# Attention stage: shorter rsqrt chains, one masking of the keys' sums, and the first choices' gating on ScalarE

## The reference, cut to what matters

```python
x = x + 0.5 * ffn(layernorm(x))     # 8 experts, top 2 of a softmax, capacity 1024 rows each
x = x + attention(layernorm(x))     # linear attention, 16 heads of 8
x = x + 0.5 * ffn(layernorm(x))
# attention:
q = elu(x @ Wq.T + bq) + 1; k = elu(x @ Wk.T + bk) + 1; v = x @ Wv.T + bv
kv = einsum('bthd,bthe->bhde', k, v)
denom = einsum('bthd,bhd->bth', q, k.sum(axis=1))
num = einsum('bthd,bhde->bthe', q, kv)
out = (num / clip(denom, 1e-6)) @ Wo.T + bo
# end of ffn: each token takes back the rows of its two experts, each by its gate
out = sum(gate[..., None] * y[topi, pos_c], axis=1)
```

## Time and profile before

| what | us |
|---|---|
| median of the three runs shown | 529.95 (525.56 to 532.13) |
| profiled execution, its own time | 536.02 |
| its span, from first to last instruction | 534.2 |
| VectorE busy | 351.1 (66%) |
| TensorE matmuls busy | 350.5 (66%) |
| ScalarE busy | 236.3 (44%) |
| GpSimd busy | 270.0 (51%) |
| mean granted clock of TensorE | 0.827 of full |

### The profile page before, as it was taken

How to read it: one execution, slowest core, us unless ns; L and a number is a source line. 1 busy time by engine, 2 the same in 40 slices (tenths; PEclk the granted TensorE clock), 3 DMA queues, 4 the chain that set the end, 5 groups by cost and what they waited for, 6 DMA issues and landing times. The chain is left out here.

```text
span 534.2 us, 6016 instructions
## 1 busy us (share of the span) xinstructions
PE 350.5 (66%) x1705; PEld 285.3 (53%) x1705; DVE 351.1 (66%) x1110; ACT 236.3 (44%) x431; POOL 270.0 (51%) x302
## 2 busy tenths in 40 slices
PE   7815568999999144887772466500088999999700
PEld 7803357888887023666651355400086888888500
DVE  6797448988887264678771585720016899999674
ACT  3685326677765022543550272310015666667400
POOL 8001765665531574554567114557720676766740
PEclk9999997999999655976785598555578999999955
DMA  8911113666652411111111001111140222321299
GB/s 244 360 48 39 51 50 121 209 224 214 222 203 88 123 51 34 39 42 34 39 48 60 17 6 41 39 41 58 58 159 1 80 83 90 88 82 44 64 341 299
DMA packets 44688, 55.22 MB, mean 103 GB/s; under 512 B 6678, under 2 KB 28208, under 8 KB 44656
## 3 DMA queue, kind: packets, MB, share of 16 engines
q1 hardware_dynamic: 31776, 35.14, 19.7%
q0 software_dynamic: 8512, 17.60, 11.4%
q10 hardware_dynamic: 4368, 2.10, 1.3%
HBM read 25.98 MB, written 28.84 MB: 103 GB/s over the span
## 5 line engine op out<-in xcount | busy, mean ns | idle before, releaser
L1060 ACT ACTIVATE hf<-psum,bcol 128x512 f32<-128x512 f32 x128 | 88.5, 692 | 74.0 <-PE psum L997 50.4
L966 POOL DMA_INDIRECT xg<-xn_dram,gidx x64 | 64.6, 1010 | 75.9 <-POOLq L1634 39.5
L956 POOL DMA_INDIRECT yt_dram<-y_sb,target x64 | 71.3, 1114 | 51.4 <-DVE y_sb L1113 30.3
L1097 DVE TENSOR_TENSOR hl<-hf,hh 128x512 fp32r<-128x512 f32 x128 | 87.7, 697 | 7.9 <-ACT hh L1062 4.7
L1202 POOL DMA_INDIRECT yg<-y_dram,slot x64 | 60.9, 951 | 62.8 <-DVE x_sb L1436 22.9
L801 POOL DMA_INDIRECT xs_dram<-xns,place x64 | 62.0, 969 | 53.2 <-DVE xns L788 34.6
L1086 DVE TENSOR_TENSOR xl<-psum,xh 128x512 fp32r<-128x512 f32 x32 | 21.9, 685 | 55.8 <-ACT xh L1045 55.8
L993 PE MATMUL psum<-xh,wres 128*128 128x512 f32 x128 | 54.3, 424 | 4.0 <-ACT xh L1045 2.7
L1008 PE MATMUL psum<-hh,wres 128*128 128x512 f32 x128 | 53.3, 416 | 0.0
L997 PE MATMUL psum<-xl,wres 128*128 128x512 f32 x128 | 51.9, 405 | 0.8 <-DVE xl L1086 0.7
L1090 DVE CAST hh<-hf 128x512 fp32r<-128x512 f32 x96 | 43.7, 455 | 11.8 <-issue 5.8
(11 more groups left out here) (232 smaller groups left out, 740.4 us busy)
## 6 DMA issues: line engine op xcount, KB each, us to landing
yt_dram<-zeros SPq DMA_DIRECT2D x24, 256.0 KB
ring<-yt_dram SPq DMA_DIRECT2D x24, 256.0 KB
xs_dram<-zeros SPq DMA_DIRECT2D x16, 288.0 KB
xg<-xs_dram SPq DMA_DIRECT2D x16, 288.0 KB
wexp_raw<-in_L_ffn_w SPq DMA_DIRECT2D x16, 256.0 KB, 6.3
y_dram<-y_sb SPq DMA_DIRECT2D x16, 256.0 KB
x_sb<-in_L_attn_x SPq DMA_DIRECT2D x8, 256.0 KB, 4.0
xn_dram<-xns SPq DMA_DIRECT2D x8, 256.0 KB, 6.1
```

The costliest lines, as they stand in the source:

```text
L956: gp.indirect_dma_start(out=yt_dram, out_offset=bass.IndirectOffsetOnAxis(ap=target[:, j:j + 1], axis=0), in_=self.y_sb[:, s % YG, t], in_ ...
L966: gp.indirect_dma_start(out=self.xg[:, s % 4, t], out_offset=None, in_=xn_dram, in_offset=bass.IndirectOffsetOnAxis(ap=gidx[:, j:j + 1], a ...
L1060: one = nc.scalar.activation(self.hf[:, c], bank[1 + c][:], ACT.Relu, bias=bcol[:, at:at + 1])
L1097: dve.tensor_tensor(self.hl[:, s % 2, c], self.hf[:, c], self.hh[:, s % 2, c].bitcast(F32), ALU.subtract).then_inc(hl_ready[c], 1)
```

## The change

Four edits, all of them around the attention stage:

1. Both rsqrt chains make one Newton turn (three instructions) and one third-order turn (four) in place of three Newton turns (nine). In the scale's chain the constants differ, as it holds minus an eighth of the root's inverse.
2. The tile of values `vv` gets 16 columns of ones in place of one, the matmul of the keys' sums has 144 columns in place of 129, `block_mask` holds the mask of the heads beside the mask of the blocks, and one instruction of 144 columns masks both. `query` waits for one signal of it, not for two.
3. ScalarE multiplies the first choices' rows of groups 1 to 7 by their gates, in place (`gated_firsts(s + 1)`, right behind `anT_out(s)`; it waits for the rows' arrival). VectorE then adds a whole group in one instruction of 512 columns, and waits for ScalarE's signal `yg_gated`. The signal that frees the rows' buffer (`yg_used[0]`) still comes from the addition. Group 0 stays as it was.
4. In VectorE's list `add_rows(s + 1, 0)` moves behind `residual(s - 2)` and `statistics(s - 2)`.

```diff
-            for turn in range(3):
-                ch.add(dve.tensor_tensor(a, y, y, ALU.mult))
+            for turn in range(2):
+                if turn == 0:
+                    ch.add(dve.tensor_tensor(a, y, y, ALU.mult))
+                else:
+                    ch.add(dve.scalar_tensor_tensor(a, y, LAST_SQUARE, y, ALU.mult, ALU.mult))
...
+                if turn == 1:
+                    ch.add(dve.scalar_tensor_tensor(a, a, LAST_SHIFT, a, ALU.add, ALU.mult))
...
-                ch.add(dve.scalar_tensor_tensor(rstd[:, ts] if turn == 2 else y, a, 1.5, y, ALU.add, ALU.mult))
+                ch.add(dve.scalar_tensor_tensor(rstd[:, ts] if turn == 1 else y, a, 1.875 if turn == 1 else 1.5, y, ALU.add, ALU.mult))
...
-                    pe.wait_ge(kv_masked, 2 * n + 2)
+                    pe.wait_ge(kv_masked, n + 1)
...
+                def gated_firsts(n):
+
+                    act.wait_ge(yg_in[0][n % YB], 64 * (n // YB + 1))
+                    for t in range(GT):
+                        at = GT * n + t
+                        y = self.yg[:, n % YB, 0, t]
+                        last = nc.scalar.activation(y, y, ACT.Identity, scale=gate[:, 0, at:at + 1])
+                    last.then_inc(yg_gated, 1)
...
                     if s < NG:
                         anT_out(s)
+                    if s + 1 < NG:
+                        gated_firsts(s + 1)
...
+                    if k == 0 and n > 0:
+                        xb = x_sb[:, GT * n:GT * n + GT]
+                        dve.wait_ge(yg_gated, n)
+                        dve.tensor_tensor(xb, self.yg[:, n % YB, k], xb, ALU.add).then_inc(yg_used[k], 1)
+                        return
...
-                    for square in (64.0, 16.0, 4.0):
+                    for square in (64.0, KEY_SQUARE):
...
-                    dve.tensor_tensor(self.kv[:, u, 0:C], bank[4][:, 0:C], block_mask[:], ALU.mult).then_inc(kv_masked, 1)
-                    dve.tensor_tensor(self.kv[:, u, C:C + HEADS], head_mask[:], bank[4][:, C:C + 1].to_broadcast([P, HEADS]), ALU.mult).then_inc(kv_masked, 1)
+                    dve.tensor_tensor(self.kv[:, u], bank[4][:, 0:C + HEADS], block_mask[:], ALU.mult).then_inc(kv_masked, 1)
...
-                    if s + 1 < NG:
-                        add_rows(s + 1, 0)
                     if s >= 2:
                         residual(s - 2)
                         statistics(s - 2)
+                    if s + 1 < NG:
+                        add_rows(s + 1, 0)
```

More of the change, by code:

```diff
@@ L58 @@
 RSQRT_SEED = 1597463007.0
+LAST_SQUARE, LAST_SHIFT = 1.2247449159622192, 2.041241407394409
+KEY_SQUARE, KEY_SHIFT = 19.595918655395508, -4.082482814788818
 NEG_EIGHTH_SEED = RSQRT_SEED - 3 * 2.0 ** 23 - 2.0 ** 31
@@ L138, in macaron @@
         head_mask = sb("head_mask", [P, HEADS])
-        block_mask = sb("block_mask", [P, P])
+        block_mask = sb("block_mask", [P, C + HEADS])
         zeros = sb("zeros", [P, GT, XW])
@@ L239, in macaron @@
         yg_used = sems("yg_used", 2)
+        yg_gated = sem("yg_gated")
         xs_cleared = sem("xs_cleared")
@@ L295, in row_scalar_steps @@
                 ch.wait(done)
-                ch.add(dve.scalar_tensor_tensor(rstd[:, ts] if turn == 2 else y, a, 1.5, y, ALU.add, ALU.mult))
+                if turn == 1:
+                    ch.add(dve.scalar_tensor_tensor(a, a, LAST_SHIFT, a, ALU.add, ALU.mult))
+                    done = ch.n
+                    yield
+                    ch.wait(done)
+                ch.add(dve.scalar_tensor_tensor(rstd[:, ts] if turn == 1 else y, a, 1.875 if turn == 1 else 1.5, y, ALU.add, ALU.mult))
                 done = ch.n
@@ L1231, in __init__ @@
                 self.kk = new("kk", [P, 2, GT, C])
-                self.vv = new("vv", [P, 2, GT, C + 1])
+                self.vv = new("vv", [P, 2, GT, C + HEADS])
                 self.kv = new("kv", [P, 2, C + HEADS])
@@ L1277, in keysum @@
                     for t in range(GT):
-                        last = nc.tensor.matmul(bank[4][:, 0:C + 1], self.kk[:, n % 2, t], self.vv[:, n % 2, t], start=(t == 0), stop=(t == GT - 1))
+                        last = nc.tensor.matmul(bank[4][:, 0:C + HEADS], self.kk[:, n % 2, t], self.vv[:, n % 2, t], start=(t == 0), stop=(t == GT - 1))
                     last.then_inc(keysum_ready, 1)
                 def query(n):
-                    pe.wait_ge(kv_masked, 2 * n + 2)
+                    pe.wait_ge(kv_masked, n + 1)
                     pe.wait_ge(qT_ready, n + 1)
@@ L1474, in scale_steps @@
                         ch.wait(done)
-                        to = self.rsa[:, u, 0] if square == 4.0 else y
-                        ch.add(dve.scalar_tensor_tensor(to, a, -3.0, y, ALU.add, ALU.mult))
+                        if square == KEY_SQUARE:
+                            ch.add(dve.scalar_tensor_tensor(a, a, KEY_SHIFT, a, ALU.add, ALU.mult))
+                            done = ch.n
+                            yield
+                            ch.wait(done)
+                            ch.add(dve.scalar_tensor_tensor(self.rsa[:, u, 0], a, 7.5, y, ALU.add, ALU.mult))
+                        else:
+                            ch.add(dve.scalar_tensor_tensor(y, a, -3.0, y, ALU.add, ALU.mult))
                         done = ch.n
@@ L1670, in _ @@
                 ch.then(nc.gpsimd.affine_select(out=head_mask[:], in_=head_mask[:], compare_op=ALU.is_ge, fill=0.0, base=HD - 1, pattern=[[HD, HEADS]], channel_multiplier=-1))
[L1671 removed]
+                ch.add(nc.gpsimd.tensor_copy(block_mask[:, C:C + HEADS], head_mask[:]))
+                ch.add(nc.gpsimd.tensor_copy(block_mask[:, 0:C].rearrange("p (h d) -> p h d", d=HD), head_mask[:].unsqueeze(2).to_broadcast([P, HEADS, HD])))
                 ch.add(nc.gpsimd.iota(iota_lo[:], pattern=[[1, P]], base=0, channel_multiplier=0, **fl))
@@ L1770, in _ @@
             def _(gp):
-                nc.gpsimd.memset(attention.vv[:, :, :, C:C + 1], 1.0).then_inc(ones_col, 1)
+                nc.gpsimd.memset(attention.vv[:, :, :, C:C + HEADS], 1.0).then_inc(ones_col, 1)
                 route1.last_column(gp)
```

## The result

The changed kernel takes 538.62 us (median of 4 runs, 537.80 to 540.53) against 531.04 us for the kernel before (4 runs, 525.56 to 538.14): ratio 1.0165, 95% interval 1.0122 to 1.0208. Without it the median before is 529.95 us, and the change costs 8.7 us. It is slower; whether by more or less than 2% the interval leaves open. The profiled execution took 539.17 us, its span is 537.4 us at a granted clock of 0.825; before it was 536.02 and 534.2. So the two traces differ by 3.2 us where the times differ by 8.7: the profiled execution of before is slower than those three runs. What a faster execution of it looks like on that chip stands in no trace.

The account below looks back on a forecast made before the run. It took attention-stage turns to be bound by a ring of GpSimd gathers and late TensorE signals. 4.8 + 2.0 - 2.0 + 1.4 - 1.0 = +5.2 us, factor 1.0097, on the median 529.95 is 535.1 us; range 522 to 543.

Parts of the forecast that it names:

- the case that I called likeliest: Whole kernel: the forecast's own case, 532 to 538 us, likeliest 535, chance 0.42.
- A sign of being wrong: Attention stage: the prediction is wrong if TensorE's keys' sums are seen at once while GpSimd gathers.
- the ring: Attention stage: addition, eight gathers and late TensorE signal close a loop, 13.15 us a turn becoming 14.35, +4.8 in all.
- The first turn: Addition for group 2: now waits for ScalarE's copy and multiplications; +2.0 us taken, bounds 0 and 4.6.
- The dispatch: First dispatch: GpSimd's wait of 1.99 us before the last four gathers goes, -2.0 us.
- Behind the stall: After the first dispatch's wait: group 7's addition and the second choices come 3.3 us later, 1.9 taken back, +1.4 us.
- Rsqrt: Shorter chains outside the ring: 0.3 us in the first routing, 0.7 in the second routing's last parts, -1.0.
- the other one of the prediction: Attention stage: the addition must follow ScalarE's copy 0.60, multiplications 1.27 and hand-over 0.05 us.
- VectorE's length as the pace: Attention stage: turns as long as VectorE's list, saving 7.8 us, 522; halfway or nothing seen, 524 to 532, chance 0.28.
- The stall at the dispatch: First dispatch: a wait costing up to 13 us goes, giving 517 to 522 us; chance 0.12.
- The stronger ring: Attention stage: the ring plus 3 us from second-routing logits held by bursts, +10.8 or +12.3, 541 to 542; chance 0.18.

Follow-up runs that it names:

- the fast chip: Either of the two chips used for the first eight follow-up runs; the kernel before takes 497 us there.
- the two small parts: Shorter rsqrt chains and the single masking only, against the kernel before: 494.21 us, ratio 0.9932.
- the slow chip: The chip used for the last four follow-up runs; the kernel before takes 536.02 us there.
- the shorter addition: Shorter rsqrt chains, single masking, one-instruction addition in old place, no gate multiplication for first choices of groups 1 to 7, against the kernel before: 535.58 us, ratio 1.0021.
- the long burst: Shorter rsqrt chains, single masking, GpSimd's gathers waiting only for the buffer they write, against the kernel before: 542.06 us, ratio 1.0143.
- the move alone: Only the first choices' addition moved behind the residual and the statistics, against the kernel before: 501.38 us, ratio 1.0077.
- the gating alone: Only ScalarE multiplying the first choices' rows and VectorE's one-instruction addition, in its old place, against the kernel before: 517.06 us, ratio 1.0399.

## Why the forecast came out as it did

I forecast 535.0 us and 1.0097 times the kernel before; it is 538.62 us and 1.0165. The time is in the range, but 0.6 us above the 532 to 538 of the case that I called likeliest, in which the forecast lay. The change costs 8.7 us where I forecast 5.2, and the cause is only half of the story.

*A sign of being wrong that came.* I had written that the prediction is wrong if the keys' sums are seen at once while GpSimd gathers. They are: they end at 230.34 and the masking starts at 230.38, while the gathers run from 223.40 to 233.15, and in the turn before at 216.06 and 216.31. What the trace bears out is narrower than that test: signals given 6.8 and 6.9 us into these bursts pass, and those given 8.3 to 9.7 us into them are seen only behind the end. So the ring closes through the projection and the transposition, and not through the masking. Nor was VectorE idle 1 to 4 us for ScalarE in these turns: it was 0.25, since the residual's own late signal came first.

*The ring.* Forecast 14.35 us a turn, measured 14.12 in the turns for groups 3 and 4. The parts: addition 0.69, hand-over 0.27, gathers 9.75, until the signal 1.62, copy 0.50 (the multiplications start 0.50 behind its start, I had counted its whole 0.60), multiplications 1.26, hand-over 0.03. So +0.97 a turn; then +1.18 for group 5 and +0.40 for group 6, in which I had counted the full 1.20 although the bound of 0 for the last two was written beside it. Measured over four turns +3.5, forecast +4.8.

*The first turn.* I took +2.0; the addition for group 2 starts at 208.32, before at 208.35: 0. I had left out that group 1's addition also waits for ScalarE, 4.68 us, and starts at 195.23 in place of 191.19; the gathers start later, `anT_out(1)` comes at 206.53, earlier than the 211.00 of the earlier trace rows, and the two cancel.

*The dispatch.* -2.0 forecast; the scatters start 1.38 us later than before, which is +3.5 less 2.1. Right. With the two errors above, 278.19 in place of my 281.6.

*Behind the stall.* +1.4 forecast; from 1.38 us later at the first dispatch to 3.75 at the second part's first scatter it is +2.4. The residual and `anT_out(6)` go on together at 302.04 and 302.09, 3.7 us behind the last scatter's end at 298.31 (before 1.1 for the residual and 3.3 for the copy), and the addition and the second choices behind them, as I had it, only later.

*Rsqrt.* -1.0 forecast; from the second part's scatters to the fourth's (354.16, before 351.32) the difference falls from 3.75 to 2.84, -0.9. Some 0.4 comes back behind them. On the fast chip, where no late signal covers the chains, the two small parts are worth 3.3 us. That is more than the 1.0 of the sum, and less than the 4.7 that it would be with 0.4 and 0.06 more in each of 8 groups.

*The sum.* +5.2 forecast, the traces give 537.44 - 534.18 = +3.3. The times give +8.7, and the interval's lower end, 1.0122, lies above my 1.0097. That 538.62 is near 535 is thus partly luck: the sum of the terms, made against one execution of a kernel whose runs spread over 12.6 us, is too small. Of the 8.7 us the traces account for 3.3; for the rest there is no trace, and which term it belongs to stays open.

*The cause.* "The ring of gathers and late signals" describes the slow chip: the turn of before, 12.71 with the shorter addition, the 12.7 us of the long burst, and the two turns of 14.12 at granted clocks of 0.96 and 0.76 fit it. As the reason for the change's price it isn't needed: on the fast chip, without one late signal, the change costs 1.82%, and with half of the gathers gone 1.28%, against 1.65% in the result. In both places the turn can come to nearly the same length, 14.12 and 14.20 us, and up to the keys' sums it is the same (they start 228.95 - 222.44 = 6.51 us behind the addition in one, 217.12 - 210.61 = 6.51 in the other). What fills it up differs: on the fast chip it is TensorE's slow matmuls, without which the turn is 11.52; on the slow one it is late signals, with 2.6 us of it beyond TensorE's own end at a clock of 0.96, and with 0.85 us where its matmuls are slow as well. That the two lengths agree is chance. The step common to both is the other one of the prediction: the addition can't start before `anT_out`, the multiplications and the hand-over. Moving the multiplications ahead of the copy took back 6.4 of 9.2 us on the fast chip. What is left there, 1.0065 against the 0.9932 of the two small parts alone, isn't taken apart; the move alone had cost 0.8%. The term that I had in no list at all is TensorE's clock, 0.76 where the turn takes 14.2 us there and 0.96 where it takes 11.5.

*The rivals.* VectorE's length as the pace was to make it faster when signals aren't late; on the fast chip they weren't, and it was slower, since the idle time before the addition isn't VectorE's length. I had weighed the wait for ScalarE against it as a matter of chance, where it decides. The stall at the dispatch stayed. The stronger ring, at 541 to 542, did not come. ScalarE, busy less than half of the span, gave 1.26 us a turn and cost VectorE up to 5.0 in the run with the gating alone. The Trainium skill (ScalarE: Activation LUTs, Rules for kernel authors) gives multiplications and additions to VectorE; by the time, the runs agree with it (1.0399 for the gating alone), though for the place of the work more than for its price, 1.26 us on ScalarE against 0.44 saved.

## What to carry to other kernels

Before work is moved to an idle engine, look at what stands ahead of it in that engine's list and what that waits for: 1.26 us of work placed behind a copy that depends on the same turn's matmuls made a loop through three engines out of an addition that had waited for neither of the other two. Then try the place before the amount: the same instructions two positions earlier in the list were 1.3% faster. And a wait for a remote signal, read from one trace, may not be the kernel's: price the change without it as well, before a forecast rests on it. Last, when two orders are compared by one turn, look at its neighbours and at the granted clock in each: here the same kernel's turn was 11.52 and then 14.20 us.

## What was unexpected of the hardware

The same kernel took 531 us beside the result, 497 us beside the first eight runs and 536 us beside the last four. Nearly the whole difference lies ahead of the last scatter: from there to the end it is 142.4 us in the earlier trace rows's execution and 141.2 in that at 497. On the slow chip signals of TensorE are often seen late, mostly 1.1 to 4.6 us behind the end of a burst of GpSimd's indirect DMAs: 2.5 us late with a burst of 9.8 us, 12.7 with one of 29.8. The tie isn't complete: a signal given early in a burst can pass, and after the change the masking at 292.89 went on in the midst of a burst that lasts from 268.19 to 298.31, behind 14.10 us of idle time. In the eight traces of the fast chip no wait from 176 to 400 us is put down to remote, with gathers at the same distance of 1.25 us; in all the traces of the slow chip, and in the two beside the result, there are some. What makes the one chip so stays open.

On the fast chip the order of the times goes with TensorE's mean granted clock from 176 to 400 us, though not in every pair: 0.77 for the kernel before and 0.75 for the two small parts and for the multiplications ahead of the copy, then 0.71 for the move alone, 0.70 for the whole change and 0.69 for the gating alone, the slowest. Cause and effect can't be told apart by this.
